# Turning the experts' weights in the DMA instead of on TensorE, for the last two of four chunks

## What is computed

```python
probs = jax.nn.softmax(xf @ Wr, axis=-1)
topk_p, topk_i = jax.lax.top_k(probs, K)                  # K = 2 of E = 16
cw = jnp.zeros((T, n_exp), x.dtype).at[jnp.arange(T)[:, None], topk_i].add(topk_p)
...
y = jax.nn.silu(xf @ wg) * (xf @ wu) @ wd
return (acc + y * c[:, None], None)                       # c: one expert's column of cw
```

## Time and profile before

| | us |
|---|---|
| median of 3 runs (lowest, highest) | 239.13 (238.85, 239.4) |
| the profiled execution, its own time | 239.48 |
| its span in the profile | 237.7 |
| PE busy (share of the span) | 226.5 (95%) |
| DVE busy | 191.1 (80%) |
| POOL busy | 182.1 (77%) |
| ACT busy | 165.1 (69%) |

### The profile page before, as it was taken

How to read it: one execution, slowest core, us unless ns; L and a number is a source line. 1 busy time by engine, 2 the same in 40 slices (tenths; PEclk the granted TensorE clock), 3 DMA queues, 4 the chain that set the end, 5 groups by cost and what they waited for, 6 DMA issues and landing times.

```text
span 237.7 us, 5815 instructions
## 1 busy us (share of the span) xinstructions
PE 226.5 (95%) x1830; PEld 166.9 (70%) x1830; DVE 191.1 (80%) x791; ACT 165.1 (69%) x333; POOL 182.1 (77%) x334
## 2 busy tenths in 40 slices
PE   7998999999999999999998999999999999999994
PEld 7775657666667675666675766677788887787872
DVE  3699897998999889999799988288756796966753
ACT  5448767789687899687975696776667559555560
POOL 6489898999898989898999979256477564666551
PEclk9999999999999999999999999999999999999999
DMA  5717914741008712017624620033324330036201
GB/s 140 224 37 181 295 61 113 201 111 69 4 0 187 199 59 48 1 22 189 170 87 137 206 98 3 0 91 133 101 86 130 123 100 0 0 132 199 95 24 44
DMA packets 16303, 24.38 MB, mean 103 GB/s; under 512 B 3281, under 2 KB 5969, under 8 KB 16145
## 3 DMA queue, kind: packets, MB, share of 16 engines
q1 hardware_dynamic: 15840, 24.01, 35.0%
q10 hardware_dynamic: 432, 0.01, 0.1%
HBM read 13.39 MB, written 1.18 MB: 61 GB/s over the span
## 4 chain that ended last, share of the span: by engine, by line
PE 68%; DVE 17%; ACT 8%; issue 3%; DMA 1%; SPq 1%; DVEq 0%; ACTq 0%
PE bank L933 68%; DVE sc L728 7%; ACT pr L413 3%; ACT h_t L355 2%; ACT xn L368 1%; DMA qk_st<-qk 1%; DVE mx L728 1%; DVE sc L897 1%; DVE qk L643 1%; DVE h_lo L676 1%; DVE qk_st L825 1%; DVE ex L689 1%; DVE stats L631 1%; DVE struck L701 1%; ACT L592 1%
## 5 line engine op out<-in xcount | busy, mean ns | idle before, releaser
L299 POOL TENSOR_SCALAR sc<-sc,mx 128x256 f32<-128x256 f32 x256 | 121.9, 492 | 8.4 <-DVE mx L728 7.1
L728 DVE CUSTOM_DVE_ANT_0 sc<-bank,decay 128x256 f32<-128x256 f32 x256 | 91.1, 420 | 10.5 <-PE bank L933 10.4
L413 ACT ACTIVATE pr<-bank 128x512 f32<-128x512 f32 x128 | 69.4, 596 | 20.7 <-PE bank L933 20.7
L933 PE MATMUL bank<-id_f,sc 128*128 128x128 f32 x512 | 69.3, 277 | 2.6 <-ACT pr L413 2.1
L343 POOL TENSOR_TENSOR act_lo<-sc,act_hi 128x512 fp32r<-128x512 f32 x35 | 45.2, 1295 | 34.6 <-ACT act_hi L583 34.6
L933 PEld LDWEIGHTS bank<-id_f,sc 128*128 128x128 f32 x512 | 55.7, 141 | 16.6 <-issue 8.1
L891 DVE TENSOR_TENSOR pr<-bank,cwb 128x512 f32<-128x512 f32 x32 | 22.1, 689 | 15.5 <-PE bank L933 15.5
L933 PE MATMUL bank<-pr,v_one 128*32 128x256 f32 x512 | 34.3, 385 | 0.0
L592 ACT ACTIVATE bank<-bank 128x512 f32<-128x512 f32 x32 | 18.7, 583 | 20.3 <-PE bank L933 20.0
L897 DVE TENSOR_TENSOR sc<-pr,bank 128x512 f32<-128x512 f32 x36 | 24.8, 688 | 5.7 <-PE bank L933 2.4
L933 PE MATMUL bank<-h_hi,wgu_hi 128*128 128x512 f32 x72 | 28.8, 400 | 0.0
(11 more groups left out here) (112 smaller groups left out, 270.4 us busy)
## 6 DMA issues: line engine op xcount, KB each, us to landing
cwb<-cw_dram SPq DMA_DIRECT2D x64, 128.0 KB, 2.9
qk_st<-qk SPq DMA_DIRECT2D x60, 128.0 KB, 2.7
wgu_sb<-in_w_gu SPq DMA_DIRECT2D x1, 1152.0 KB, 5.4
wgu_sb<-in_x_t SPq DMA_DIRECT2D x4, 256.0 KB, 4.0
x_all<-in_x SPq DMA_DIRECT2D x1, 768.0 KB, 7.6
o_sum<-o_t SPq DMA_DIRECT2D x6, 128.0 KB, 2.1
o_val<-o_t SPq DMA_DIRECT2D x6, 128.0 KB, 2.1
out_dram<-wgu_sb SPq DMA_DIRECT2D x3, 256.0 KB, 3.1
```

The costliest lines, as they stand in the source:

```text
L299: last = nc.gpsimd.tensor_scalar(sc[:, n % RING, t, :], sc[:, n % RING, t, :], -1.0, mx[:, n % RING, t:t + 1], ALU.mult, ALU.add)
L413: nc.scalar.activation(pr[:, n % RING, :, :].rearrange("p a b -> p (a b)"), turn_bank(i, n)[:], ACT.Exp, scale=-1.0).then_inc(s["exp_done" ...
L728: last = nc.vector.tensor_tensor_reduce(sc[:, n % RING, t, :], ps_s[n % SB][:, t * SEQ:t * SEQ + SEQ], decay[:, t, :], float(HD) ** -0.5, ...
L933: return nc.tensor.matmul(o, l, r, start=start, stop=stop, skip_group_check=not check, is_transpose=transpose or None)
```

## The change

Chunks 2 and 3 no longer go through `weights_turn` and `weights_take`. SP writes `cw` to `cw_dram` itself, with four DMAs for a chunk, one for each tile of 128 tokens. Each writes its 128 x 16 numbers transposed: neighbours in a partition of `cw` go to rows of `cw_dram` that are 2048 bytes apart, so every number is a piece of 4 bytes. These writes count on a semaphore of their own, `cw_turned`, for which the loads of that chunk wait. Since `cw` is now read by a DMA, `r_keep` of chunk 3 waits until chunk 2's has landed. `router_exp` of chunk 3 moves from unit 19 to unit 18, and `route_c` from unit 21 to unit 19. PE's wait for `x2_ok`, which stood before the removed transposes of unit 6, stands before `ln2t` in unit 12 now.

```diff
             def weights_out(c):
-                sp.wait_ge(s["cwt_ok"], c + 1)
-                sp.dma_start(cw_dram[c], cw_t[:]).then_inc(s["cw_out"], 16)
+                if c < NCHUNK - 2:
+                    sp.wait_ge(s["cwt_ok"], c + 1)
+                    sp.dma_start(cw_dram[c], cw_t[:]).then_inc(s["cw_out"], 16)
+                    return
+                sp.wait_ge(s["cw_ok"], c + 1)
+                with nc.allow_non_contiguous_dma("expert weights turned on their way"):
+                    for t in range(TT):
+                        sp.dma_start(cw_dram[c, :, t * P:t * P + P].rearrange("e p -> p e"),
+                                     cw[:, t, :]).then_inc(s["cw_turned"], 16)
...
-                        if u == 0:
+                        if u == 0 and c + 1 < NCHUNK - 2:
                             sp.wait_ge(s["cw_out"], 16 * (c + 2))
+                        elif u == 0:
+                            sp.wait_ge(s["cw_turned"], 16 * TT * (c + 4 - NCHUNK))
                         weights_in(c + 1, u)
...
-                        if u == 6:
-                            weights_take(c - 1)
...
                     if i == 2:
-                        if u == 1:
+                        if u == 0:
                             router_exp(c)
-                        if u == 5:
-                            weights_take(c)
...
             def r_keep(c):
                 dve.wait_ge(s["struck_ok"], c + 1)
+                if c == NCHUNK - 1:
+                    dve.wait_ge(s["cw_turned"], 16 * TT)
...
-                    if i == 2 and u == 3:
+                    if i == 2 and u == 1:
                         route_c(c)
...
-                        if u == 6:
-                            pe.wait_ge(s["x2_ok"], c + 1)
-                            weights_turn(c - 1)
                     if i == 1:
                         if u == 3:
-                            pe.wait_ge(s["cwt_ok"], c)
+                            pe.wait_ge(s["x2_ok"], c + 1)
                             ln2t(c)
...
-                    if i == 2 and u == 5:
-                        pe.wait_ge(s["lg_ok"], c + 1)
-                        weights_turn(c)
```

More of the change, by code:

```diff
@@ L132, in build @@
             "h2t_ok h2hi_ok h2lo_ok r_done lg_ok top_ok fill_ok ls_ok struck_ok ex_ok zs_ok rz_ok em_ok "
-            "cw_ok cwt_done cwt_ok cw_out "
+            "cw_ok cwt_done cwt_ok cw_out cw_turned "
             "gate_done up_done silu_done mul_done act_ok ahi_ok alo_ok down_done "
```

## The result

The changed kernel takes **292.6 us** in the median (287.4 to 306.4), against 239.3 us for the kernel before on the same chip: a ratio of 1.210 with a 95% interval of 1.205 to 1.216, **slower by some 50 us**. The mechanism is that of the slower rival, at several times the size that its text gave as the likely one, 243.3 us.

What follows compares the result with a forecast made beforehand. PE was taken to bound the kernel, busy 95% and without gaps in the feed-forward part. The sum 239.13 - 0.44 - 0.78 + 1.08 + 0 = 239.0 us meant no change; the range was 237.8 to 247 us.

Steps and rivals of the forecast that it cites:

- the slower rival: Turned write outlasts its cover, over 11.3 us: unit 27's multiply late, PE stalls 4.3 us at unit 29, 243.3 us; chance 34%.
- What is added: two writes in pieces of 4 bytes: Chunks 2 and 3: 512 pieces per engine at 8.8 ns plus 2.1 us to land, 6.6 us a chunk, all hidden.
- the row of like size: ACT queue's 432 small load packets, 0.1% of 16 x 237.7 us, taken as 8.8 ns a piece.
- the far end of that step: A chunk's write at 31.4 us, bounded from the load of x_all at 3.6 ns a piece over all engines.
- The cover: Chunk 3's write may last 11.3 us, 18 ns a piece, before unit 27 at no cost; beyond, each us costs one.
- Its far end: A write of 31.4 us loses 20 us at chunk 3 and some 10 more at unit 18: about 269 us.
- Chunk 2's cover: Write issued in unit 7, wanted in unit 18: eleven units, 23 us, before anything waits.
- What is removed: PE's transposes: chunk 2's in unit 6 save 0.44 us, chunk 3's in unit 23 save 0.78 with their wait, together 1.22.
- The new stall at unit 22: Moved routing and late silu fall on one activation; both blocked by POOL, PE stalls 1.08 us before unit 22's up product.
- The faster rival: The two blockings beside POOL don't both recur, activation 20 is just in time, no stall: 237.9 us; chance 22%.
- The sum without the write: Whole kernel: savings of 0.44 and 0.78 us, stall of 1.08 us, write costing 0: 239.0 us.

Runs made afterwards that it cites:

- the probes: Kernel before, plus single-tile writes of 4-byte pieces at varied distances, and other forms, timed one by one behind its last output; its own time says nothing.
- chunk3_only: Changed kernel, but chunk 2's weights turned by PE as before and without r_keep's wait; only chunk 3 turned by DMA: 282.1 us, ratio 1.178.
- own_line: Changed kernel with the same 4-byte pieces, each number 64 bytes from its neighbours in a tensor nothing reads; loads take chunk 1's rows: 242.9 us, ratio 1.016.
- rows_write: Changed kernel with each of the four writes untransposed, as 128 pieces of 64 bytes, so weights reach wrong tokens: 239.27 us, ratio 0.9994.
- pitch_2560: Changed kernel with rows of cw_dram 2560 bytes apart instead of 2048, same DMAs otherwise: 271.6 us, ratio 1.135.
- the read-back: Kernel before with cw written as rows and read back turned, replacing PE's transposes: chunk 2 alone 239.11 us; chunks 0 to 2, chunk 3's transposes later, 238.95 us.

## Why the prediction was wrong

*The step that failed* is the size of "What is added: two writes in pieces of 4 bytes". It took 512 pieces for each engine at 8.8 ns, by the row of like size, and 6.6 us in all. Measured were 49.6 and 39.8 us. Even the far end of that step, 31.4 us, was too low. The row itself is rough: 0.1% is printed to one digit, so 8.8 ns may be 4.4 to 13; that alone would not have broken the forecast. The row was like in the size of the packets and unlike in what decides. It is a row of loads, and the changed kernel writes; its packets went to different places, and here sixteen numbers from sixteen partitions go into the same 64 bytes. Loads of the same small size are cheap here as well: 8192 of them took 9.5 us, which is (9.5 - 2.1) / 512 = 14 ns each by the prediction's formula. Writes that share nothing take (13.1 - 2.1) / 512 = 21 ns, and with the sharing it is 74 to 93 ns. The cover would have borne 18. So the forecast falls by the plain write already, and by the sharing it falls far.

*What spoke for it in the text* was the Trainium skill, "DMA: Bandwidth & Descriptors", sections "Specifications" and "Rules for kernel authors", which warn of writes under 512 bytes and of a strided last dimension. Their direction is borne out: a tile took 1.7 us in pieces of 64 bytes and 4.2 at least in pieces of 4. Whether 512 bytes are a limit for the size of a piece no run here shows. What the probes vary is the distance between pieces of 4 bytes: 6.8 us for a tile at 32 bytes, 5.0 at 64 and 4.2 at 512. I had set the rule aside because no row bore on it; with a cost that no row of the trace shows, and a rule that says it is large, 34% for the slower rival and an upper end of 247 us were too little.

*The slower rival's mechanism* was right throughout: DVE waits for `cwb<-cw_dram` in unit 27, and in unit 18 too, and PE stands two units later. Its far end had "20 us there, and some 10 more for chunk 2". With 39.8 and 49.6 us put into the same formulas it would have given 39.8 - 11.3 = 28.5 (29.7 measured) and 49.6 - 31.4 + 10 = 28 (28.2 measured).

*The cover of 11.3 us* held: 11.1 by `chunk3_only`, 13.24 - 2.21 = 11.0 by `own_line`. In the changed kernel, where chunk 2's write had made everything late and unit 22 didn't stall, it was 39.8 - 29.7 = 10.1, less by that stall, which was a part of the cover. Chunk 2's cover was 49.6 - 28.2 = 21.4 us, a little less than the eleven units or 23 us of the text.

*What is removed* held. In `rows_write` the matmul that answers to 166.92 starts at 165.78, 1.14 us earlier, for reasons in the attention part; unit 22's up product would have started at 200.23, 1.57 us before 201.80. The difference is 0.43 us, and 0.44 was the forecast. From unit 22's up product to the last matmul are 232.63 - 201.23 = 31.40 us, of which 0.10 belong to the stall, and it was 233.88 - 201.80 = 32.08 us: 0.78 us less, as forecast for chunk 3's transposes and their wait.

*The new stall at unit 22* held to 0.02 us (1.10 against 1.08), by the cause given: L721 at 0.95 and L727 at 1.22 us beside POOL. In the changed kernel the same two met POOL otherwise, and took 0.43 and 0.22 us:

```profile
226.88 0.43 DVE L721 SCALAR_TENSOR_TENSOR cw<-struck,ex 128x64 f32<-128x64 f32 x1
227.34 0.22 DVE L727 TENSOR_TENSOR cw<-cw,rz 128x64 f32<-128x64 f32 x1
...
225.94 2.78 POOL L352 TENSOR_TENSOR act_lo<-sc,act_hi 128x512 fp32r<-128x512 f32 x2 [28.96 <-ACT act_hi L592]
```

POOL's two subtractions last 1.29 and 1.35 us. The first ends at 227.23, and L721, begun 0.35 us earlier, ends at 227.31. The second starts only at about 227.4, since its rounded activation was not there sooner, and L727 has begun before it and isn't held up. That is the order that the faster rival asked for: with no subtraction ready, L727 takes its 0.22 us.

*The faster rival* had its condition fail in `rows_write`: both blocked. In the changed kernel it held, but only behind a hole of 28 us. *The sum without the write* was right: 239.0 us forecast, 239.27 measured with the write made short.

*Not foreseen* is that PE comes out of each hole at half its clock, 4.5 us in all. The holes of `chunk3_only` and `pitch_2560` cost 1.6 to 2.7 us each in this way.

*What stays open:* why the same turned write takes 16 us one time and 33 the next; why rows of 2560 bytes are cheaper than 2048 when pieces share 64 bytes; what makes shared 64 bytes slow, since the runs show the price and not its mechanism; and whether the read-back gains anything in the attention part.

## What to carry to other kernels

A DMA's cost is not read from its bytes or from its number of pieces alone: ask where neighbouring pieces land, and whether several of them write into the same 64 bytes. If an array has to be turned between SBUF and DRAM, write it in its own order and turn it on the read: here 12.1 us for the write and the turned read together (13.6 with the write of `cw_t` behind them), against 40 to 51. And where a cost is in no row of the trace, and there is a rule that says that it is large, let the bound go well beyond the nearest row and give the case its weight.

## What the runs showed of the hardware

- Writes of 4 bytes into DRAM, 2048 in one DMA: 4.2 to 5.0 us when each has 64 bytes or more to itself, 6.8 to 7.0 with neighbours 32 bytes apart, 9.6 to 11.2 with 8 from one partition, 17.3 to 18.6 when four to eight partitions write into the same 64 bytes and 15.5 to 32.7 when sixteen do, in rows 2048 bytes apart (11.4 and 15.0 with 2560); the same bytes as rows of 64 take 1.7.
- Four such DMAs together take less than four times one: 51.9 us where one is 16 to 33, and, in the kernel, 13.1 where one alone is 4.2. With shared 64 bytes the length of a row counts: 32.5 us with 2560 bytes, and in the kernel 28.6 to 29.7 against 39.8 to 51.1.
- Turned reads of 4 bytes: 8192 in 9.5 us.
- PE at 0.50 of its clock for eleven matmuls of 512 columns (4.7 to 4.9 us) after standing for 28 to 30 us; for eight after 40.0 us (`chunk3_only`), ten after 10.2 and thirteen after 18.4 (`pitch_2560`), so their number doesn't follow the length of the hole. After 2.2 us (`own_line`) the steps are 0.33 us once and then 0.23 to 0.24: the granted clock stays 1.00.
- Of two VectorE instructions in a row beside GpSimd subtractions without a gap, each waits for the end of one: 0.95 and 1.22 us (`rows_write`). Begun 0.04 us ahead of a subtraction, the second takes 0.22 (the changed kernel).
